# A new order of the pipeline step in a fused attention and ternary feed-forward kernel

## Chip, cores and metric

The kernel runs on one core of one Trainium2 chip. The metric is the device time of one execution in microseconds (us); less is better. The inputs and weights lie in the chip's main memory when the time starts, and the result is there when it ends.

## The reference

```
# x, ctx: (16, 128, 256) f32; 16 heads of 16; hidden width 1024
def attention(q, k, v):                    # k = v = ctx
    Q, K, V = heads(q @ Wq.T), heads(k @ Wk.T), heads(v @ Wv.T)
    p = softmax(Q @ K.T / 4, axis=-1)
    return merge(p @ V) @ Wo.T
def ffn(x):
    h = bit_linear(x, w1)                  # token rounded to 8 bits, weight to -1, 0, 1
    h = silu(conv3_over_tokens(h) + b)     # each hidden channel by itself
    return bit_linear(h, w2)
x = x + tanh(g_xattn) * attention(layernorm(x), ctx, ctx)
x = x + tanh(g_ffn)   * ffn(layernorm(x))
```

The token rounding takes the largest absolute value of a token (row) as 127. The weight rounding takes one mean absolute value for the whole matrix.

## The kernel before

Sixteen sequences of 128 tokens go through one hand-written software pipeline. Every engine has its own queue, written out in one block per engine; the queues meet in semaphores alone. The unit is a step `s` (`step` at L573 for TensorE, L837 for ScalarE, L1062 for VectorE, the loop at L367 for GpSimd). In a step four sequences are at work, with these names: b = s has its scores formed, n = s + 1 is projected, a = s - 1 is weighed with its values, d = s - 2 is normalised and rounded for the feed-forward part.

**TensorE's order in a step** (L573): `project_out(d)` (attention output times Wo, L506), `project_v(n)` (L417), `weigh(a)` (probabilities times values, L480), `x_transpose(n)` (L397), `max_transpose(b)` (row maxima, L434), `int_transpose(d-1)` (rounded tokens and their scales, L513), `project_q(n)` (L426), `unweighted_transpose(a)` (L494), the first of two hidden tiles (`hidden`, L544), `row_stage(b, 0)`, the second hidden tile, `att_transpose(a)` (L500), `project_k(n+1)` (L404), `row_stage(b, 1)`. A row stage (L441) has half of the scores of b and, between them, half of the unshifted scores of n, from which VectorE takes the row maxima. Row stage 1 waits for the exponent of row stage 0 and for VectorE's `row_max(n, 1)`, because it writes over both banks. All matrices of the attention are f32, which takes two passes a product; the profile counts each pass.

**ScalarE's order** (L837): `exponent(a, 1)` (L786), any extra work, `middle_tap` of both tiles of the step before (L817), `v_copy(n)` (L775), `sum_x`, `x_copy(n)` (L760), `u_copy(a)` (L791), `int_copy(d-1)` (two copies, L801), `q_copy(n)` (L781), `square_x`, `raw_copy` of the first tile (L812), `exponent(b, 0)`, `att_copy(a)` (L796), `k_copy(n+1)` (two copies into a buffer of keys, L765).

**VectorE's order** (L1062): `row_max(b, 0)` (L982), `residual1(d)` with the statistics of the second layernorm (L1009), `outer_taps` of one tile (L1037), `shift_q(b)` (L990), `outer_taps` of the other tile, `normalise(a)` (L1001), `row_max(n, 1)`, `quantise1(d)` (largest value and its inverse, L1019), `dequantise` of the second tile (L1029). **GpSimd's order** (L367): `norm2(d)` (L321), `dequantise` of the first tile (L345), `round1(d)` (L333), `norm1(n+1)` (L300), `x_mean` (L296).

**Hidden tiles.** From step 6 on two tiles of 128 hidden channels by 512 tokens are made per step (`TILES`, L46). The even tile is copied to SBUF by ScalarE (`raw`, L143) and multiplied with the token scales by GpSimd; the odd one VectorE multiplies out of PSUM. `ps_xqT`, `ps_deq`, `ps_w2sum` and `ps_h` lie in one bank (L159 to L174), so a hidden tile waits until `int_copy` has read its part (L564), and step 7 (`SUMS_STEP`, L47) adds the column sums of w2 in the same bank (L532), which `w2_sums_copy` (L833) takes out. Keys have three buffers (L120), values three (`VB`).

**Ends.** Before step 1 a written-out start (L637 to L662) fills the pipeline, with `project_k(2)` ahead of `row_stage(0, 1)`. The mean absolute values of w1 and w2 are summed by ScalarE in steps 1 to 4 (L903); VectorE rounds w1 and w2 in quarters (`ternary`, L1047) in steps 3 to 6, two a step, and TensorE waits before step 5 for the second mean (`mean_done`, L681). Step 15 is `last_step` (L610, L870, L1085); behind it comes a written-out mix of tiles, silu, token rounding and the second product. `keep_busy` (L392) is a product of identity matrices whose result nobody reads.

## Time and profile before

| | |
|---|---|
| Median of three runs | 236.19 us (236.08 to 236.39) |
| The profiled execution, its own time | 237.18 us |
| Its span in the profile | 235.2 us |
| Busy share: TensorE, VectorE, ScalarE, GpSimd | 92%, 81%, 69%, 52% |
| Chain that ended last: TensorE, VectorE, ScalarE | 68%, 21%, 3% |
| TensorE's granted clock, mean | 0.984 of full speed |

The span is the stretch from the first to the last instruction. A busy share is an average over stages with different limits: steps 1 to 14 last from 19.1 to 153.9 us, the last step and the written-out end from there to 235.2 us. The chain follows the work that ended last back to what released it. The stretches below are given in us from the span's start, and an instruction's duration can overlap the next one's on the same engine, so the distance of two starts tells what an instruction costs its queue.

### The profile page before, as it was taken

To read this page: it belongs to the slowest core of one execution; us is meant where nothing else is said; L and a number is where in the kernel's file an instruction comes from. 1 tells how busy PE (TensorE), PEld (TensorE's weight loads), DVE (VectorE), ACT (ScalarE), POOL (GpSimd) and SP (SyncE) were. 2 spreads that over 40 slices of the span, in tenths; PEclk is the share of its full clock that TensorE was granted. 3 is DMA by queue.
4 is the path that set the end of the run, shared out by engine and by line. 5 is a ranking of instruction groups with operands and counts; after the bars stand their busy time and mean duration, and the time that the engine had idled before them with its cause. 6 is when DMAs were issued, how large, how long until landed. Compare 5 with 4: busy or idle time off the path is not lost.

```text
span 235.2 us, 6424 instructions
## 1 busy us (share of the span) xinstructions
PE 215.8 (92%) x2439; PEld 180.1 (77%) x2452; DVE 190.4 (81%) x387; ACT 161.9 (69%) x318; POOL 122.2 (52%) x229
## 2 busy tenths in 40 slices
PE   7999999997999999999999999989985699997974
PEld 7887787886878787887878878768783588886963
DVE  4163548789798999999999999999899859999671
ACT  2557768777687888989889788667933356674741
POOL 2421326364365757668677576657567224433470
PEclk9999999999999999999999999999999589999999
DMA  5982011010110101100000000000000000111111
GB/s 168 370 270 67 3 49 38 10 46 3 45 47 3 46 3 45 40 11 22 3 3 3 3 0 3 1 3 0 3 0 0 24 25 22 47 46 45 49 52 60
DMA packets 9488, 9.86 MB, mean 42 GB/s; under 512 B 1010, under 2 KB 9202, under 8 KB 9458
## 3 DMA queue, kind: packets, MB, share of 16 engines
q1 hardware_dynamic: 9458, 9.46, 12.2%
q8 instruction: 19, 0.31, 0.6%
q14 instruction: 11, 0.09, 0.1%
HBM read 7.36 MB, written 2.10 MB: 40 GB/s over the span
## 4 chain that ended last, share of the span: by engine, by line
PE 68%; DVE 21%; issue 5%; ACT 3%; DMA 1%; POOL 1%; SPq 0%; ACTq 0%; DVEq 0%; POOLq 0%
PE ps_score L464 10%; PE ps_proj L430 8%; PE ps_proj L509 6%; PE ps_av L487 6%; PE ps_max L474 6%; PE ps_proj L422 5%; DVE zmax L1151 5%; PE ps_proj L413 4%; PE ps_h L568 4%; PE ps_av L707 4%; DVE y L1041 4%; DVE y L1044 3%; DVE smax L987 3%; PE ps_av L497 2%; PE ps_proj L401 2%
## 5 line engine op out<-in xcount | busy, mean ns | idle before, releaser
L987 DVE TENSOR_REDUCE smax<-ps_max 128x8 f32<-128x1024 f32 x31 | 37.9, 1223 | 13.9 <-PE ps_max L474 10.7
L789 ACT ACTIVATE prob<-ps_score 128x1024 f32<-128x1024 f32 x32 | 32.7, 1023 | 17.8 <-PE ps_score L464 16.9
L464 PE MATMUL ps_score<-Qs,KT 32*128 32x128 f32 x512 | 37.1, 283 | 2.0 <-DVE smax L987 0.8
L464 PEld LDWEIGHTS ps_score<-Qs,KT 32*128 32x128 f32 x512 | 31.3, 186 | 9.3 <-issue 5.0
L474 PE MATMUL ps_max<-KT,QT 32*128 32x256 f32 x248 | 35.1, 400 | 0.0
L359 POOL TENSOR_SCALAR zq<-y,zmax 128x1024 f16<-128x1024 f32 x16 | 17.9, 1119 | 29.1 <-issue 18.1
L1151 DVE TENSOR_REDUCE zmax<-y 128x1 f32<-128x1024 f32 x16 | 19.4, 1214 | 5.3 <-ACT y L935 5.3
L336 POOL TENSOR_SCALAR xn<-xn,qa 128x256 f32<-128x256 f32 x16 | 8.1, 508 | 28.1 <-DVE qa L1027 28.1
L829 ACT ACTIVATE y<-hid,conv 128x512 f32<-128x512 f32 x24 | 18.6, 807 | 4.3 <-DVE hid L1034 3.9
L707 PE MATMUL ps_av<-w2q,zqT 128*128 128x256 f16 x128 | 17.4, 281 | 4.3 <-ACT zqT L941 2.6
L474 PEld LDWEIGHTS ps_max<-KT,QT 32*128 32x128 f32 x248 | 21.1, 184 | 0.1
L1044 DVE SCALAR_TENSOR_TENSOR y<-hid,conv,y 128x508 f32<-128x508 f32 x24 | 19.6, 818 | 0.8
L941 ACT ACTIVATE zqT<-ps_proj 128x512 f32<-128x512 f32 x16 | 9.6, 598 | 15.2 <-PE ps_proj L696 15.2
L430 PE MATMUL ps_proj<-xnT,wq 128*128 128x128 f32 x128 | 18.3, 286 | 0.9 <-ACT xnT L763 0.6
L509 PE MATMUL ps_proj<-wo,attT 128*128 128x256 f32 x64 | 18.1, 405 | 1.1 <-DVE w_mean L1124 1.1
L1041 DVE SCALAR_TENSOR_TENSOR y<-hid,conv,y 128x508 f32<-128x508 f32 x24 | 18.7, 778 | 0.0
L430 PEld LDWEIGHTS ps_proj<-xnT,wq 128*128 128x128 f32 x128 | 15.6, 191 | 3.7 <-ACT xnT L763 3.5
L770 ACT ACTIVATE KT<-ps_proj,shift_row,head_mask 128x256 f32<-128x256 f32 x32 | 16.3, 563 | 2.5 <-PE ps_proj L413 2.5
L707 PEld LDWEIGHTS ps_av<-w2q,zqT 128*128 128x128 f16 x128 | 12.1, 101 | 7.2 <-DVE xres L1161 4.9
L487 PE MATMUL ps_av<-prob,V 128*32 128x128 f32 x512 | 17.3, 276 | 0.1
L350 POOL TENSOR_TENSOR hid<-raw,deq 128x512 f32<-128x512 f32 x10 | 13.1, 1311 | 7.9 <-ACT raw L815 7.9
L487 PEld LDWEIGHTS ps_av<-prob,V 128*32 128x32 f32 x512 | 13.0, 110 | 5.4 <-issue 4.5
(140 smaller groups left out, 551.9 us busy)
## 6 DMA issues: line engine op xcount, KB each, us to landing
cin<-ctxT SPq DMA_DIRECT2D x16, 128.0 KB, 2.1
xres<-x SPq DMA_DIRECT2D x16, 128.0 KB, 2.5
out<-xres SPq DMA_DIRECT2D x16, 128.0 KB, 1.7
w1f<-w1T SPq DMA_DIRECT2D x1, 1024.0 KB, 6.2
w2f<-w2T SPq DMA_DIRECT2D x1, 1024.0 KB, 8.1
wk<-wkT SPq DMA_DIRECT2D x1, 256.0 KB, 2.8
wv<-wvT SPq DMA_DIRECT2D x1, 256.0 KB, 4.4
wq<-wqT SPq DMA_DIRECT2D x1, 256.0 KB, 4.6
```

The source lines that it names most:

```text
L430: mm = pe.matmul(ps_q[:, t * P:(t + 1) * P], wq[:, k * D + t * P:k * D + (t + 1) * P], xnT[:, k * P:(k + 1) * P], start=(k == 0), stop=(k ...
L464: mm = pe.matmul(ps_score[:, i * 512 + j * P:i * 512 + (j + 1) * P], KT[b % 3][rows, j * P:(j + 1) * P], Qs[rows, j * P:(j + 1) * P], star ...
L474: mm = pe.matmul(into[:, i * 512 + t * 2 * P:i * 512 + (t + 1) * 2 * P], QT[n % 2][rows, t * P:(t + 1) * P], KT[n % 3][rows, t * 2 * P:(t ...
L487: mm = pe.matmul(ps_av[g * ROW:(g + 1) * ROW, j * P:(j + 1) * P], V[a % VB][:, h * ROW:(h + 1) * ROW], prob[g // PG][:, (g % PG * GH + j) ...
L509: mm = pe.matmul(ps_o, attT[:, t * P:(t + 1) * P], wo[:, t * D:(t + 1) * D], start=(t == 0), stop=(t == KD - 1))
L707: pe.matmul(ps_f, zqT[v % 2][:, c * P:(c + 1) * P], w2q[:, c * D:(c + 1) * D], start=(c == 0), stop=False)
L789: act.activation(prob[pair][:, :], ps_score[:, :], ACT.Exp, scale=DH ** -0.5).then_inc(exp_done, 1)
L829: act.activation(y_tile(T), by_sequence(hid[T % HB][:, :]), ACT.Identity, bias=conv[:, 4 * c + 3:4 * c + 4], scale=conv[:, 4 * c + 1:4 * c ...
L987: dve.tensor_reduce(dst, first_max(n, pair)[:, :].rearrange("p (g t e k) -> p g t e k", g=PG, t=KD, e=2), AX.X, ALU.max).then_inc(max_done, 1)
L1041: dve.scalar_tensor_tensor(y3[:, :, 1:P], h3[:, :, 0:P - 1], conv[:, 4 * c:4 * c + 1], y3[:, :, 1:P], ALU.mult, ALU.add).then_inc(tap0_don ...
L1044: dve.scalar_tensor_tensor(y3[:, :, 0:P - 1], h3[:, :, 1:P], conv[:, 4 * c + 2:4 * c + 3], y3[:, :, 0:P - 1], ALU.mult, ALU.add).then_inc( ...
L1151: dve.tensor_reduce(m[:, 0:1], z[v], AX.X, ALU.max, apply_absolute_value=True).then_inc(zmax_step, 1)
```

## The change

Keys go first and the output projection last. TensorE's step becomes `project_k(n)`, `x_transpose(n)`, `int_transpose(d-1)`, `weigh(a)`, `max_transpose(b)`, `project_q(n)`, `unweighted_transpose(a)`, tile, `row_stage(b, 0)`, tile, `att_transpose(a)`, `project_v(n)`, `project_out(a)`, `row_stage(b, 1)`. So the output projection works on a = s - 1, one step earlier, and `residual1(a)` ends VectorE's step. Keys and values have two buffers each. GpSimd multiplies both tiles of a step (all tiles under 19), from two buffers `raw`, so ScalarE copies both tiles. The absolute values of w1 are summed by VectorE in step 1 instead of by ScalarE, and the quarters of `ternary` are spread over steps 2 to 6. In step 7 the column sums come ahead of `weigh`. The gates' load and the load of Wo move up in SyncE's queue. The last step is rewritten in the same manner, with `keep_busy` in two places.

```diff
-VB = 3
+VB = 2
+KB = 2
...
-        KT = [sb(f"KT{i}", [P, KD * 2 * P]) for i in range(3)]
+        KT = [sb(f"KT{i}", [P, KD * 2 * P]) for i in range(KB)]
...
-            return T % 2 == 0 and T < FIRST_LATE
+            return T < FIRST_LATE - 1
 
         def gp_tiles(T):
-            return (min(T, FIRST_LATE) + 1) // 2
+            return min(T, FIRST_LATE - 1)
 
...
             load_x(0)
+            sp.dma_start(gate_row[:, :], gates).then_inc(gate_in, 16)
             load_w(wv, wvT, KD, wv_in)
             load_w(wq, wqT, KD, wq_in)
             load_x(1)
             load_c(1)
-            sp.dma_start(gate_row[:, :], gates).then_inc(gate_in, 16)
             load_x(2)
             load_c(2)
+            load_w(wo, woT, KD, wo_in)
             load_w(w1f, w1T, KD, w1_in)
             load_x(3)
             load_c(3)
             load_w(w2f, w2T, NC_, w2_in)
-            load_w(wo, woT, KD, wo_in)
...
                 if seq(s - 2):
                     norm2(s - 2)
-                for T in TILES.get(s, ()):
+                    round1(s - 2)
+                tiles = TILES.get(s, ())
+                for T in tiles[0:1]:
+                    dequantise(T)
+                if seq(s + 2):
+                    norm1(s + 2)
+                for T in tiles[1:2]:
                     if on_gp(T):
                         dequantise(T)
-                if seq(s - 2):
-                    round1(s - 2)
-                if seq(s + 2):
-                    norm1(s + 2)
                 if seq(s + 3):
                     gp.wait_ge(sh1_done, s + 3)
...
             def project_v(n):
-                pe.wait_ge(k_done, max(n + 1, 2))
+                if n == 0 or n == 2:
+
+                    pe.wait_ge(k_done, max(n + 1, 2))
...
-                if seq(d):
-                    project_out(d)
-                if seq(n):
+                if s == 1:
                     project_v(n)
-                if seq(a):
-                    weigh(a)
-                if seq(n):
-                    x_transpose(n)
-                max_transpose(b)
+                else:
+                    project_k(n)
+                x_transpose(n)
                 if s == SUMS_STEP:
                     w2_column_sums()
                 elif seq(d - 1):
                     int_transpose(d - 1, min(tiles, default=0))
-                if seq(n):
-                    project_q(n)
+                weigh(a)
+                max_transpose(b)
                 if s == SUMS_STEP:
                     int_transpose(d - 1, min(tiles))
-                if seq(a):
-                    unweighted_transpose(a)
+                project_q(n)
+                unweighted_transpose(a)
                 between()
                 for T in tiles[0:1]:
                     hidden(T, s - 2)
                 row_stage(b, 0)
                 for T in tiles[1:2]:
                     hidden(T, s - 2)
-                if seq(a):
-                    att_transpose(a)
-                if seq(n + 1):
-                    project_k(n + 1)
-                else:
-                    pe.wait_ge(v_done, NB)
-                    keep_busy(4, ps_k)
+                att_transpose(a)
+                if s > 1:
+                    project_v(n)
+                project_out(a)
                 row_stage(b, 1)
 
             def last_step():
                 b, a, d = NB - 1, NB - 2, NB - 3
                 T, U_ = TILES[b]
-                project_out(d)
                 hidden(T, LAST)
+                int_transpose(d - 1, T)
+                keep_busy(4, ps_av)
                 weigh(a)
                 max_transpose(b)
-                int_transpose(d - 1, T)
                 unweighted_transpose(a)
                 row_stage(b, 0)
                 y_transpose(0)
                 hidden(U_, LAST)
                 att_transpose(a)
+                keep_busy(3, ps_av)
+                project_out(a)
                 row_stage(b, 1)
...
             project_k(2)
             keep_busy(2, ps_av)
             row_stage(0, 1)
-            pe.wait_ge(gate_in, 16)
-            pe.wait_ge(ones_done, 1)
-            pe.matmul(ps_setup[:, 0:2], ones[0:1, :], gate_row[:, :], start=True, stop=True).then_inc(gate_ready, 1)
+            pe.wait_ge(wo_in, 16)
             step(1)
-            pe.wait_ge(wo_in, 16)
 
...
                 act.wait_ge(k_ready, n + 1)
-                wait(act, score_ready, PG * NP * (n - 2))
-                wait(act, max_ready, PG * NP * (n - 2))
+                wait(act, score_ready, PG * NP * (n - KB + 1))
...
-                last = TILES.get(s - 1, ())
-                if seq(a):
-                    exponent(a, 1)
-                extra()
-                for T in last:
+                exponent(a, 1)
+                if s > 1:
+                    k_copy(n)
+                x_copy(n)
+                u_copy(a)
+                for T in TILES.get(s - 1, ())[1:2]:
                     middle_tap(T)
-                if seq(n):
+                if s == 1:
                     v_copy(n)
-                if seq(n + 2):
-                    sum_x(n + 2)
-                if seq(n):
-                    x_copy(n)
-                if seq(a):
-                    u_copy(a)
                 if s == SUMS_STEP:
                     w2_sums_copy()
                 if seq(d - 1):
                     int_copy(d - 1)
-                if seq(n):
-                    q_copy(n)
+                q_copy(n)
                 if seq(n + 1):
                     square_x(n + 1)
                 for T in tiles[0:1]:
                     raw_copy(T)
+                if seq(n + 2):
+                    sum_x(n + 2)
                 exponent(b, 0)
-                if seq(a):
-                    att_copy(a)
-                if seq(n + 1):
-                    k_copy(n + 1)
+                att_copy(a)
+                for T in tiles[1:2]:
+                    raw_copy(T)
+                for T in tiles[0:1]:
+                    middle_tap(T)
+                if s > 1:
+                    v_copy(n)
+                extra()
 
             def last_step():
                 b, a, d = NB - 1, NB - 2, NB - 3
                 before, now = TILES[b - 1], TILES[b]
                 exponent(a, 1)
-                middle_tap(before[0])
                 raw_copy(now[0])
+                int_copy(d - 1)
                 u_copy(a)
                 middle_tap(before[1])
-                int_copy(d - 1)
                 exponent(b, 0)
+                att_copy(a)
                 middle_tap(now[0])
-                att_copy(a)
                 exponent(b, 1)
 
 
...
-            step(1, weight_sum(0, 0))
-            act.wait_ge(gate_ready, 1)
-            act.activation(gate[:, :], ps_setup[:, 0:2], ACT.Tanh).then_inc(gate_done, 1)
-            step(2, weight_sum(0, 1))
+            step(1)
+            step(2, weight_sum(0))
             act.wait_ge(mean_done, 1)
-            step(3, weight_sum(1, 0))
-            step(4, weight_sum(1, 1))
+            step(3, weight_sum(1))
+            step(4)
             step(5, first_weights(0))
...
-                tiles, last = TILES.get(s, ()), TILES.get(s - 1, ())
-                if seq(b):
-                    row_max(b, 0)
-                if seq(d):
-                    residual1(d)
+                last = TILES.get(s - 1, ())
+                row_max(b, 0)
                 for T in last[0:1]:
                     outer_taps(T)
                 extra(0)
                 shift_q(b)
+                if seq(d):
+                    quantise1(d)
+                if seq(a):
+                    normalise(a)
                 for T in last[1:2]:
                     outer_taps(T)
-                if seq(a):
-                    normalise(a)
                 if seq(n):
                     row_max(n, 1)
-                if seq(d):
-                    quantise1(d)
-                for T in tiles[1:2]:
-                    dequantise(T)
                 extra(1)
+                if seq(a):
+                    residual1(a)
 
             def last_step():
                 b, a, d = NB - 1, NB - 2, NB - 3
                 before, now = TILES[b - 1], TILES[b]
                 row_max(b, 0)
-                residual1(d)
                 outer_taps(before[0])
                 shift_q(b)
+                quantise1(d)
+                normalise(a)
                 outer_taps(before[1])
-                normalise(a)
-                quantise1(d)
+                remainder(d - 1)
                 dequantise(now[1])
-                remainder(d - 1)
+                residual1(a)
                 outer_taps(now[0])
...
+            def first_sums(k):
+                if k == 0:
+                    dve.wait_ge(w1_in, 16)
+                dve.tensor_reduce(abs_sum[:, 2 * k:2 * k + 1], w1f[:, k * HID:(k + 1) * HID], AX.X, ALU.add,
+                                  apply_absolute_value=True).then_inc(abs_done[0], 1)
+
+            step(1, first_sums)
...
-            step(2, lambda k: weight_scale(0) if k == 1 else None)
-            step(3, pieces(0, w1f, w1q, 0, wq1_step, w1q_done))
-            step(4, pieces(2, w1f, w1q, 0, wq1_step, w1q_done, scale=1))
-            step(5, pieces(0, w2f, w2q, 1, wq2_step, w2q_done))
+            w1_args = (w1f, w1q, 0, wq1_step, w1q_done)
+            w2_args = (w2f, w2q, 1, wq2_step, w2q_done)
+
+            def second(k):
+                if k == 1:
+                    weight_scale(0)
+                    ternary(0, *w1_args)
+
+            def third(k):
+                ternary(1 + k, *w1_args)
+
+            def fourth(k):
+                if k == 0:
+                    ternary(3, *w1_args)
+                else:
+                    weight_scale(1)
+                    ternary(0, *w2_args)
+
+            def fifth(k):
+                ternary(1 + k, *w2_args)
+
+            def sixth(k):
+                if k == 0:
+                    ternary(3, *w2_args)
+
+            step(2, second)
+            step(3, third)
+            step(4, fourth)
+            step(5, fifth)
             dve.wait_ge(small_in, 16)
-            step(6, pieces(2, w2f, w2q, 1, wq2_step, w2q_done))
+            step(6, sixth)
...
-            residual1(NB - 2)
...
```

The hunks left out change only the waits that go with this (buffers, the bank of the hidden tiles, the order at the start: the gates' product and its `Tanh` now come before `project_q(0)`), and behind the last step `hidden(20)` goes first, with four `keep_busy` products ahead of `weigh(NB - 1)`.

## Rows read from the trace of the kernel before

**Rows 1.** Stretches cut at the starts of steps 2, 7 and 8:

```profile
27.68:75.75 48.07, 45.63 (x597) 38.11 (x594) 38.16 (x88) 36.13 (x82) 22.70 (x51) 1.00 0.10 29
75.75:86.47 10.72, 10.20 (x132) 8.38 (x129) 10.21 (x20) 8.61 (x20) 7.24 (x13) 1.00 0.09 27
```

**Rows 2.** Timeline of TensorE (start, length, idle before) in step 10, a steady one:

```profile
105.74 1.13 PE L509 MATMUL ps_proj<-wo,attT 128*128 128x256 f32 x4
...
107.66 1.08 PE L487 MATMUL ps_av<-prob,V 128*32 128x128 f32 x32
...
108.95 0.38 PE L438 MATMUL ps_score<-ident,smax 128*128 128x128 f32 x2
...
109.58 0.97 PEld L430 LDWEIGHTS ps_proj<-xnT,wq 128*128 128x128 f32 x8 [0.22 <-ACT xnT L763]
110.58 0.60 PE L497 MATMUL ps_av<-ident,U 128*128 128x128 f32 x4
...
111.54 0.38 PE L464 MATMUL ps_score<-Qs,KT 32*128 32x128 f32 x2
...
113.30 1.06 PE L413 MATMUL ps_proj<-cin,wk 128*128 128x128 f32 x8
114.28 0.38 PE L464 MATMUL ps_score<-Qs,KT 32*128 32x128 f32 x2
...
115.37 0.48 PE L509 MATMUL ps_proj<-wo,attT 128*128 128x256 f32 x1
```

**Rows 3.** Waits of TensorE, summed (us, times, longest):

```profile
PE ps_proj L509 <- DVE w_mean L1124: 1.1, 1, 1.1
```

**Rows 4.** Timeline of ScalarE in step 10:

```profile
106.87 1.51 ACT L829 ACTIVATE y<-hid,conv 128x512 f32<-128x512 f32 x2
...
109.43 0.59 ACT L794 ACTIVATE U<-ps_av 128x512 f32<-128x512 f32 x1
...
110.17 0.38 ACT L809 ACTIVATE deq<-ps_h,w_mean 128x128 f32<-128x128 f32 x1
110.78 0.38 ACT L784 ACTIVATE QT<-ps_proj 128x256 f32<-128x256 f32 x1 [0.23 <-PE ps_proj L430]
...
112.85 1.02 ACT L789 ACTIVATE prob<-ps_score 128x1024 f32<-128x1024 f32 x1 [0.60 <-PE ps_score L464]
```

**Rows 5.** Timelines of SyncE, TensorE and ScalarE at the start:

```profile
4.11 0.33 SPq L268 DMA_DIRECT2D gate_row<-gates  x1
...
19.10 1.13 PE L422 MATMUL ps_proj<-wv,cin 128*128 128x256 f32 x4
...
17.58 1.02 ACT L770 ACTIVATE KT<-ps_proj,shift_row,head_mask 128x256 f32<-128x256 f32 x2
...
19.22 1.02 ACT L789 ACTIVATE prob<-ps_score 128x1024 f32<-128x1024 f32 x1 [0.62 <-PE ps_score L464]
```

**Rows 6.** Timeline of GpSimd in step 10:

```profile
106.22 0.19 POOL L307 TENSOR_SCALAR var<-x_squares 128x1 f32<-128x1 f32 x1
...
108.36 0.51 POOL L323 TENSOR_SCALAR var<-mv 128x1 f32<-128x1 f32 x1
...
110.48 0.97 POOL L330 TENSOR_SCALAR xn<-xres,rstd,shift 128x256 f32<-128x256 f32 x1
...
114.80 0.48 POOL L336 TENSOR_SCALAR xn<-xn,qa 128x256 f32<-128x256 f32 x1 [1.20 <-DVE qa L1027]
```

**Rows 7.** VectorE's search for the token maximum, step 10:

```profile
113.90 0.41 DVE L1021 TENSOR_REDUCE qa<-xn 128x1 f32<-128x256 f32 x1
```

**Rows 8.** GpSimd's multiplications, shortest, median and longest (ns):

```profile
L350 POOL TENSOR_TENSOR hid<-raw,deq x10: 1266/1269/1692, 72.7 to 159.6; 128x512 f32<-128x512 f32 x10
```

**Rows 9.** Timeline of VectorE in the last step and behind it:

```profile
155.18 0.48 DVE L1011 SCALAR_TENSOR_TENSOR xres<-ps_proj,gate,xres 128x256 f32<-128x256 f32 x1
...
156.25 0.71 DVE L1041 SCALAR_TENSOR_TENSOR y<-hid,conv,y 128x508 f32<-128x508 f32 x1
...
166.69 1.22 DVE L1151 TENSOR_REDUCE zmax<-y 128x1 f32<-128x1024 f32 x1 [0.47 <-ACT y L935]
```

47 lines of the change are left out of this document (22 added, 25 removed).

## The prediction

> **What bounds the kernel now.** I read the share of busy time and the chain that ended last first: TensorE has most of both. Then the stretches step by step, because an average hides which step has room: steps 2 to 6 take 48.07 us together, though no hidden tile is made before step 6, and step 7 takes 10.72 [rows 1]. Then TensorE's timeline in a steady step, where the distance of two starts is what a stage costs. It reads: output projection with values 1.92, `weigh` with `x_transpose` 1.29, both small transposes up to the queries 0.63, queries 1.00, the U transpose with a tile 0.96, row stage, tile and `att_transpose` 1.76, keys 0.98, row stage 1.09; 9.63 in all [rows 2]. The only wait in it is 0.2 before the queries, for ScalarE's copy [rows 2]. So TensorE's own work is 9.43, and in steps 6 and 8 to 14 an order alone can give back 0.2 a step. The room is earlier, where 1.1 is one wait for the second weight mean [rows 3].
>
> I split the sums so: a pass of a 128-column transpose is 0.11, so four for U 0.44, two for the maxima 0.22, `int_transpose` 0.21, `att_transpose` 0.22, `x_transpose` 0.28; the first tile 0.52, the second 0.44, `row_stage(b, 0)` 1.10, values or output projection 0.96 each, `weigh` 1.01.
>
> **How the new step runs.** Count from the start of `project_k(n)`. ScalarE gets a product some 0.04 after its modelled end (queries: 110.58 is the next start, 110.78 the copy's) [rows 2, 4].
>
> *Steps 8 to 14.* `weigh` ends at 0.98 + 1.29 + 0.21 = 2.48. TensorE comes to the first tile at 2.48 + 0.22 + 1.00 + 0.44 = 4.14. But the tile shares its bank with what `int_copy` reads, and ScalarE now has `u_copy`, a middle tap and both int copies between the end of `weigh` and the tile: 0.11 to hand over, 0.74 for U and the first int copy, 0.75 for the tap (half of 1.51), 0.38 for the scales, 0.05 back, in all 2.03 [rows 4]; ready at 4.51. A wait of 0.37 that the old order did not have, since there V, xT and the taps lay ahead of `weigh`'s end. After it nothing is late: `att_copy` follows the exponent, 0.21 + 1.02 + 0.38 = 1.61 after the row stage [rows 4], against tile, transpose and values, 1.62. The step is 9.43 + 0.37 = 9.80, 0.17 over the old one; seven of them **+1.2**.
>
> *Steps 2 to 6.* Without a tile TensorE is at `project_out(a)` 1.18 after the row stage, but the copy needs 1.61: 0.43 wait. The copied queries come 0.20 + 0.38 + 0.05 after their product, 0.63 against 0.44: 0.19 wait. Steps 3 and 5: 2.48 + 0.22 + 1.00 + 0.63 + 1.10 + 1.61 + 0.96 + 1.09 = 9.09. Step 2 has no `int_transpose` but the weight mean (four passes, 0.44) in place of the query wait, 9.13; step 4 both, 9.34; step 6 has tiles but no tap yet, 9.43. Together 46.08 against 48.07: **-2.0**. More than half is the second mean, which now comes ahead of a `ternary` and not behind it [rows 3].
>
> *Step 7.* The column sums (eight passes, 0.9 after `project_k`'s eight) go ahead of `weigh`, and `int_transpose` has to wait until they are copied out. `weigh` ends at 3.17, then U 0.5, the tap 0.75, the copy 0.38 and the two hand-overs: 4.96. TensorE is there at 3.39 and stands 1.57. 9.43 + 0.9 + 1.57 = 11.90 against 10.72 [rows 1]: **+1.2**.
>
> *Step 1.* Two key buffers: `k_copy(2)` writes the buffer of sequence 0 and so waits for all its scores, the event that started the exponent at 19.22; before it ran at 17.58 [rows 5]. It comes first in ScalarE's queue, so it ends at 20.24, and `project_v(2)`, which waits for it and stood at 19.10, starts at 20.29. The exponent and `weigh` queue behind. From there 0.96 + 1.29 + 0.22 + 1.00 + 0.63 + 1.10 + 1.61 + 0.96 + 1.09 = 8.86, so step 2 starts at 29.15 and not at 27.68: **+1.5**. Each step now holds `project_out(a)` where the old one held `project_k(n+1)`, so the two starts compare like with like.
>
> *GpSimd.* It gets a second multiplication, 1.27 and 0.1 between instructions [rows 8]. Its round of one step: `norm1` and mean 2.14, `norm2` 3.09 (110.48 + 0.97 - 108.36), VectorE's `quantise1` for which it stands still 0.90, `round1` 1.05 (114.80 to the next `norm1`, 9.63 behind 106.22), two multiplications 2.74 [rows 6 to 8], with a hand-over 10.0. That is 0.2 over TensorE's 9.80. Lower bound nothing, as `quantise1` has slack before the row maximum that TensorE needs; upper 7 times 0.2. I take half, **+0.7**. `norm1` stays early enough for `x_transpose`: it has nearly a step of cover.
>
> *VectorE* gives up a multiplication and is covered. w1's sums go to it in step 1, where it is idle half the time; should w1 come late the shift would stand behind them, for which no row speaks. *ScalarE* gets a copy of 0.6 and still has idle time.
>
> *Loads.* The gates' issue takes 0.33 of SyncE's queue [rows 5] and moves ahead of wv, wq, x1 and c1; Wo's moves ahead of w1. All are awaited later than they land, so nothing; were the cover of x1 gone, 0.33. The gates' product moves from the front of step 1 to an idle place: nothing.
>
> *The end.* `residual1(13)`, 1.07 of VectorE (155.18 to 156.25), leaves the last step, so `shift_q(15)` comes up to that earlier; I take 0.6, because the four `keep_busy` products hold `weigh` back. But three more and `project_out(14)` now stand ahead of `row_stage(15, 1)`: 0.73 (six of the passes of keys) and 0.96. The exponent, the table load and the first silu hang on that stage, and VectorE's first token maximum waited for silu already, at 166.69 [rows 9]. Later by 1.69 - 0.6 = **+1.1**; bounds 0.6 and 1.7, and -1.07 if VectorE's work alone sets the end.
>
> **The sum:** 1.5 - 2.0 + 1.2 + 1.2 + 0.7 + 1.1 = +3.7. The profiled execution's span of 235.2 becomes 238.9 and its own 237.18 becomes 240.9; it lies 1.0 over the median of the runs shown, to which I add the same: 236.19 + 3.7 = **239.9**. Its own range, with half of each wait and the bounds of the end and of GpSimd: 237.5 to 242.
>
> **Where a rule of the skill bears on it.** GpSimd's multiplication took 1.27 nearly always, and 1.69 the one time that VectorE's taps ran beside it (159.6) [rows 8]; the scaling in `norm2` shows 0.97 under a tap [rows 6]. The Trainium skill (SBUF — State Buffer, Who interferes with whom) says why: a VectorE instruction with two SBUF inputs and a GpSimd one that reads SBUF lock each other out for the whole instruction. The trace agrees with its direction. By it the second multiplication is dearer than an idle GpSimd makes it look, and the taps can stand behind it too.
>
> **Rivals.**
> 1. *The lock makes GpSimd the bound* (0.14). If one multiplication a step lasts 1.69, the round is 10.0 + 0.42 = 10.4; seven steps at 0.64 over 9.80 are 4.5 in place of 0.7: 243.7. For it: new places beside the taps. Against: `norm2` then meets fewer taps, and the maxima have PSUM inputs. It decides from the point where the round is over 9.8.
> 2. *Faster: ScalarE's copies are never late in steps 2 to 14* (0.19). Its queue has 0.6 idle before the exponent [rows 4], and if the chain from `weigh` to the tile takes under 1.66 and not 2.03, TensorE runs packed: 8.70, 8.47, 8.91, 8.47 and 9.43 for steps 2 to 6 (-4.1), step 7 10.33 (-0.4), 9.43 for seven steps (-1.4). With step 1 and the end, +1.5 and +1.1, that is -3.3: 232.9. For it: 0.37 is a small difference of two sums. Against: each term is a row's length, and the exponent with its copy takes 1.61 whatever the queue does.
> 3. *It cancels* (0.07): the end is paid by VectorE's work (-1.07 for +1.1) and step 7's copy is not late (0 for +1.2): 3.7 - 2.2 - 1.2 = +0.3, 236.5.
>
> **How the numbers follow.** The forecast has 0.60. A measurement of this kernel tells 0.2% (0.5 us) from no change. Faster: rival 2 and a seventh of rival 3, 0.20; same: the rest of rival 3 less a little, 0.05; slower 0.75. The range from 235.9 to 243.0 holds the forecast, rival 3 and the lower part of rival 1 and leaves out rival 2, some 0.2.
>
> **What the new profile would show.** Right: `project_v(2)` at 20.3 and `k_copy(2)` after the scores; step 7 close to 11.9 with TensorE idle before `int_transpose`; steady steps of 9.8 to 10.0 with the wait before the first tile on ScalarE's scale copy; no wait on the weight mean; silu(0) later against the start of step 15. Wrong: steady steps under 9.63, or a tile that waits for nothing; then the ScalarE chain is mis-sized. GpSimd without idle time but for `quantise1` would speak for rival 1.

## The result, and the profile after

The changed kernel takes 241.53 us (median of four runs, 241.27 to 241.62) against 236.29 for the kernel before on the same chip. The ratio is 1.0213, 95% interval 1.0185 to 1.0241: slower by 5.2 us. The profiled execution of the changed kernel took 241.27 with a span of 239.5, 4.3 over the span before.

Page of the changed kernel: busy shares, the chain that ended last, the group of GpSimd's multiplications (count, busy us, mean ns, idle before).

```profile
PE 214.4 (90%) x2453; PEld 177.8 (74%) x2466; DVE 187.3 (78%) x378; ACT 163.5 (68%) x323; POOL 133.8 (56%) x238
...
PE 63%; DVE 19%; issue 8%; ACT 7%; DMA 1%; POOL 1%; SPq 0%; ACTq 0%; DVEq 0%; POOLq 0%
...
L351 POOL TENSOR_TENSOR hid<-raw,deq 128x512 f32<-128x512 f32 x19 | 26.8, 1409 | 1.0 <-ACT raw L814 0.9
```

TensorE has lost share of the chain, and ScalarE and "issue" have gained it: TensorE works as long as before but stands more often. A view by stretch says where. These are the changed kernel's stretches, cut at `project_v(2)` and at the starts of steps 2, 7, 8 and 15 (stretch, length, then busy time and count of PE, PEld, DVE, ACT and POOL, granted clock, DMA share, GB/s).

```profile
20.68:29.64 8.96, 7.71 (x106) 6.12 (x106) 5.92 (x9) 4.59 (x11) 1.77 (x5) 1.00 0.11 31
29.64:76.21 46.57, 45.22 (x598) 37.23 (x595) 39.47 (x90) 36.18 (x82) 25.36 (x56) 1.00 0.11 30
76.21:88.45 12.24, 10.52 (x132) 8.26 (x129) 9.44 (x17) 9.32 (x21) 7.65 (x14) 1.00 0.09 25
88.45:158.35 69.90, 66.00 (x844) 52.65 (x849) 58.13 (x112) 58.81 (x127) 55.56 (x88) 1.00 0.04 11
```

Against [rows 1]: steps 2 to 6 take 46.57 in place of 48.07, step 7 12.24 in place of 10.72. The last row holds seven steps of 9.98; before they took 9.63. Next TensorE's timeline in step 1, in the steady step that starts at 108.42, and in step 7 (start, length, idle before and its releaser).

```profile
20.68 1.10 PE L427 MATMUL ps_proj<-wv,cin 128*128 128x256 f32 x4 [1.37 <-ACT KT L769]
...
27.49 1.13 PE L512 MATMUL ps_proj<-wo,attT 128*128 128x256 f32 x4 [1.13 <-ACT attT L798]
...
81.28 0.27 PE L533 MATMUL ps_h<-ident,xq 128*128 128x128 bf16 x2 [1.45 <-issue]
...
110.96 0.44 PE L443 MATMUL ps_score<-ident,smax 128*128 128x128 f32 x2
111.23 1.06 PE L435 MATMUL ps_proj<-xnT,wq 128*128 128x128 f32 x8
112.12 0.60 PE L500 MATMUL ps_av<-ident,U 128*128 128x128 f32 x4
113.05 0.11 PEld L572 LDWEIGHTS ps_h<-xqT,w1q 128*128 128x128 bf16 x2 [0.56 <-ACT deq L808]
113.28 0.38 PE L572 MATMUL ps_h<-xqT,w1q 128*128 128x512 bf16 x1 [0.56 <-ACT deq L808]
```

The last of these lines needs care. A tile is two passes, and the line holds one (x1): this trace has no record of the first pass, in any of steps 8 to 14. Its weight load shows when the tile really started, at 113.05. In the trace of experiment 5, whose steps are as long, both passes are recorded, and the wait reads 0.33 and not 0.56:

```profile
113.71 0.60 PE L573 MATMUL ps_h<-xqT,w1q 128*128 128x512 bf16 x2 [0.33 <-ACT deq L809]
```

The forecast new waits are all there: the values behind `k_copy(2)`, the output projection behind `att_copy`, `int_transpose` in step 7 behind the sums' copy (the view names no releaser, experiment 2 shows it), the first tile behind the scale copy. One was not forecast. At the end of step 7 row stage 1 waits for VectorE's row maxima, which stand behind a tap that met a multiplication of GpSimd and took 1.64 in place of 0.75:

```profile
87.36 0.38 PE L467 MATMUL ps_score<-Qs,KT 32*128 32x128 f32 x2 [0.22 <-DVE smax L983]
...
84.44 1.64 DVE L1040 SCALAR_TENSOR_TENSOR y<-hid,conv,y 128x508 f32<-128x508 f32 x1
...
84.14 1.39 POOL L351 TENSOR_TENSOR hid<-raw,deq 128x512 f32<-128x512 f32 x1 [0.94 <-ACT raw L814]
```

And ScalarE's side of two of the forecast waits:

```profile
19.52 1.02 ACT L769 ACTIVATE KT<-ps_proj,shift_row,head_mask 128x256 f32<-128x256 f32 x2 [1.66 <-PE ps_score L467]
20.43 1.02 ACT L788 ACTIVATE prob<-ps_score 128x1024 f32<-128x1024 f32 x1
...
111.17 0.60 ACT L793 ACTIVATE U<-ps_av 128x512 f32<-128x512 f32 x1 [0.26 <-PE ps_av L490]
111.67 0.80 ACT L828 ACTIVATE y<-hid,conv 128x512 f32<-128x512 f32 x1
112.37 0.37 ACT L806 ACTIVATE xqT<-ps_h 128x256 bf16<-128x256 bf16 x1
112.64 0.37 ACT L808 ACTIVATE deq<-ps_h,w_mean 128x128 f32<-128x128 f32 x1
112.89 0.39 ACT L783 ACTIVATE QT<-ps_proj 128x256 f32<-128x256 f32 x1
```

In the first two lines the keys' copy waits for the scores and holds the exponent back, where [rows 5] had the copy at 17.58 and the exponent at 19.22. In the others U, the tap and two copies run without a gap, and TensorE waits for the second copy. GpSimd in the same step:

```profile
108.14 1.27 POOL L351 TENSOR_TENSOR hid<-raw,deq 128x512 f32<-128x512 f32 x1
...
113.11 0.48 POOL L337 TENSOR_SCALAR xn<-xn,qa 128x256 f32<-128x256 f32 x1 [1.11 <-DVE qa L1023]
...
114.53 1.69 POOL L351 TENSOR_TENSOR hid<-raw,deq 128x512 f32<-128x512 f32 x1
```

One of the two multiplications takes 1.69 in each of steps 8 to 13, as the one under a tap had [rows 8]. The only idle time is 1.11 for the token maximum. Where GpSimd is the bound (experiment 10) that wait is 0.93, so by these two rows I estimate 0.18 to spare here. Last, the first token maximum behind the last step, which was at 166.69 [rows 9]:

```profile
172.37 1.22 DVE L1169 TENSOR_REDUCE zmax<-y 128x1 f32<-128x1024 f32 x1 [2.28 <-ACT y L931]
```

From there the changed kernel needs 67.1 us to the end of its span and the kernel before 68.5. The clock says why. TensorE alone, the kernel before first, then the changed one (stretch, length, busy, granted clock, DMA share, GB/s):

```profile
184.00:188.00 4.00, 3.60 (x17) 0.50 0.11 35
188.00:192.00 4.00, 4.00 (x27) 0.72 0.01 2
```

```profile
184.00:188.00 4.00, 2.47 (x23) 1.00 0.00 0
188.00:192.00 4.00, 1.92 (x11) 0.68 0.00 0
192.00:196.00 4.00, 4.00 (x32) 0.89 0.11 37
```

Around the start of the second product TensorE falls to 1.2 GHz (0.50) for a while; before it lay idle for most of 180 to 184 (1.09 busy of 4.00). The stretch at the lower clock was shorter in this execution after the change. The profiled kernel with two multiplications below (experiment 10) has the long one, 68.4 us from the token maximum to the end, and its partner with one multiplication the short one, 67.2. So some 1.2 us of the difference of two single spans can be this.

### The profile page after: what moved, and what is told of

Its sections match the earlier page's. It is cut to its first block, busy times and chain, and to the rows that moved or that the text cites. A ratio compares the mean times of both kernels' runs of the same rounds, so it can differ in the third digit from the quotient of the medians.

```text
span 239.5 us, 6464 instructions
## 1 busy us (share of the span) xinstructions
PE 214.4 (90%) x2453; PEld 177.8 (74%) x2466; DVE 187.3 (78%) x378; ACT 163.5 (68%) x323; POOL 133.8 (56%) x238
## 4 chain that ended last, share of the span: by engine, by line
PE 63%; DVE 19%; issue 8%; ACT 7%; DMA 1%; POOL 1%; SPq 0%; ACTq 0%; DVEq 0%; POOLq 0%
PE ps_score L467 10%; PE ps_av L490 7%; PE ps_proj L416 7%; PE ps_proj L512 6%; PE ps_max L477 5%; DVE zmax L1169 5%; DVE y L1037 4%; PE ps_proj L427 4%; PE ps_h L572 4%; DVE y L1040 4%; PE ps_proj L435 3%; PE ps_av L707 3%; ACT y L828 2%; DVE xres L1179 2%; PE ps_av L398 2%
## 5 line engine op out<-in xcount | busy, mean ns | idle before, releaser
L351 POOL TENSOR_TENSOR hid<-raw,deq 128x512 f32<-128x512 f32 x19 | 26.8, 1409 | 1.0 <-ACT raw L814 0.9
L828 ACT ACTIVATE y<-hid,conv 128x512 f32<-128x512 f32 x24 | 19.5, 814 | 4.9 <-DVE hid L1030 3.9
L707 PE MATMUL ps_av<-w2q,zqT 128*128 128x256 f16 x128 | 16.6, 273 | 4.3 <-ACT zqT L937 2.6
L1040 DVE SCALAR_TENSOR_TENSOR y<-hid,conv,y 128x508 f32<-128x508 f32 x24 | 18.9, 788 | 0.9
L991 DVE SCALAR_TENSOR_TENSOR Qs<-ps_score,max_row,QT 128x256 f32<-128x256 f32 x32 | 14.0, 477 | 6.5 <-PE ps_score L443 6.4
L1037 DVE SCALAR_TENSOR_TENSOR y<-hid,conv,y 128x508 f32<-128x508 f32 x24 | 18.9, 786 | 0.0
L416 PE MATMUL ps_proj<-cin,wk 128*128 128x128 f32 x128 | 18.3, 286 | 0.0
L427 PE MATMUL ps_proj<-wv,cin 128*128 128x256 f32 x64 | 16.5, 381 | 1.4 <-ACT KT L769 1.4
L435 PE MATMUL ps_proj<-xnT,wq 128*128 128x128 f32 x128 | 17.0, 275 | 0.0
```

What stands on the lines that cost most here:

```text
L351: gp.tensor_tensor(hid[T % HB][:, :], raw[T % 2][:, :], deq[:, G * GT:(G + 1) * GT], ALU.mult).then_inc(scaled_gp, 1)
L416: mm = pe.matmul(ps_k[:, t * P:(t + 1) * P], wk[:, k * D + t * P:k * D + (t + 1) * P], cin[n % CB][:, k * P:(k + 1) * P], start=(k == 0), ...
L427: mm = pe.matmul(ps_v, cin[n % CB][:, k * P:(k + 1) * P], wv[:, k * D:(k + 1) * D], start=(k == 0), stop=(k == KD - 1))
L1037: dve.scalar_tensor_tensor(y3[:, :, 1:P], h3[:, :, 0:P - 1], conv[:, 4 * c:4 * c + 1], y3[:, :, 1:P], ALU.mult, ALU.add).then_inc(tap0_don ...
L1040: dve.scalar_tensor_tensor(y3[:, :, 0:P - 1], h3[:, :, 1:P], conv[:, 4 * c + 2:4 * c + 3], y3[:, :, 0:P - 1], ALU.mult, ALU.add).then_inc( ...
```

## The experiments

All ratios are against the kernel before, run beside it on the same chip (its medians there lie between 236.29 and 236.85). The table reads, for each kernel: start of step 2, length of step 7, length of each of steps 8 to 14, start of the first token maximum, median time. Its first four columns come from TensorE's and VectorE's timelines; the beginning of the program shifts by up to 0.7 from one execution to the next (`project_k(2)` starts between 16.55 and 17.27). So two kernels are best compared by the distance from the start of step 2 to the token maximum, 142.73 in the changed kernel.

| kernel | step 2 | step 7 | steps 8 to 14 | token max | median | ratio |
|---|---|---|---|---|---|---|
| before | 27.68 | 10.72 | 9.63 | 166.69 | 236.29 | 1 |
| after | 29.64 | 12.24 | 9.98 | 172.37 | 241.53 | 1.0213 |
| 1 three keys | 28.21 | 12.24 | 9.98 | 170.92 | 240.36 | 1.0197 |
| 2 sums' copy first | 29.72 | 10.63 | 9.98 to 10.32 | 172.08 | 241.37 | 1.0224 |
| 3 scales before tap | 30.09 | 11.66 | 9.80 to 10.31 | 172.96 | 242.18 | 1.0248 |
| 4 row stage first | 29.66 | 12.24 | 9.98 | 171.72 | 241.05 | 1.0205 |
| 5 one multiplication | 30.29 | 12.24 | 9.98 | 173.01 | 241.84 | 1.0220 |
| 6 = 2, 3 and 5 | 30.16 | 10.46 | 9.81 | 169.87 | 239.35 | 1.0110 |
| 7 = 1 to 5 | 28.45 | 10.46 | 9.81 | 167.51 | 236.78 | 1.0018 |
| 8 old step, two mult. | 28.16 | 12.14 | 10.81 to 11.23 | 178.90 | 248.82 | 1.0497 |
| 9 = 7, tap after queries | 28.89 | 11.11 | 9.47 to 9.76 | 167.79 | 236.92 | 1.0027 |
| 10 = 9, two mult. | 28.18 | 11.11 | 9.75 to 10.29 | 169.68 | 239.89 | 1.0153 |
| 11 = 9, maxima first | 28.41 | 10.63 | 9.47 to 9.76 | 166.86 | 236.11 | 0.9990 |
| 12 = 11, tap after raw | 28.55 | 10.35 | 9.48 | 165.24 | 234.13 | 0.9888 |

**1. Keys in three buffers again.**

```diff
-KB = 2
+KB = 3
```

> The new kernel with three key buffers instead of two. Theory: with two, k_copy(2) waits for all scores of sequence 0 and project_v(2) stands 1.37 us for it; with three that wait is gone, project_v(2) starts near 19.4 in place of 20.7, all later stages are 1.2 to 1.4 earlier with steps of unchanged length, and the time is 240.2 (0.5% less than the new kernel's 241.5). Rival: the first step is held by the exponent and its att_copy (1.13 before project_out(0)) whatever the keys do; then step 2 starts where it did, near 29.6, and the time stays at 241.5.

Measured: 240.36 us, ratio 1.0197 (1.0142 to 1.0252), 1.2 under the changed kernel. `project_v(2)` starts at 19.20, step 2 at 28.21 and not 29.64, and all later steps keep their lengths. The missing buffer is the cause of that part of step 1, and it is paid once. The trace shows this and the ratio doesn't, since its interval holds 1.0213: one of the four executions took 242.57.

**2. The column sums' copy ahead of U's in step 7.**

```diff
                 x_copy(n)
+                if s == SUMS_STEP:
+                    w2_sums_copy()
                 u_copy(a)
...
-                if s == SUMS_STEP:
-                    w2_sums_copy()
```

> The new kernel with the copy of w2's column sums ahead of u_copy and the middle tap in ScalarE's queue of step 7. Theory: TensorE's wait of 1.45 before int_transpose in step 7 is this copy standing behind U and the tap; ScalarE is idle for 0.91 just where the copy now goes, so the wait goes, about 0.4 comes back before the first tile as in a steady step, step 7 takes 11.0 to 11.2 and not 12.24, time 240.4. Rival: the step is held by VectorE or GpSimd (quantise1 waits there too), then step 7 stays over 11.9 and the time at 241.3 or more.

Measured: 241.37 us (1.0224, 1.019 to 1.0258), no gain. Step 7 fell from 12.24 to 10.63, as it should, but steps 10 to 13 rose to 10.20 to 10.32. GpSimd in a step of 10.3 of that kernel:

```profile
117.73 1.28 POOL L351 TENSOR_TENSOR hid<-raw,deq 128x512 f32<-128x512 f32 x1
118.98 0.67 POOL L299 TENSOR_SCALAR minus_mean<-x_total 128x1 f32<-128x1 f32 x1
119.73 0.68 POOL L324 TENSOR_SCALAR var<-mv 128x1 f32<-128x1 f32 x1
...
124.44 1.69 POOL L351 TENSOR_TENSOR hid<-raw,deq 128x512 f32<-128x512 f32 x1
```

The two operations on 128x1 took 0.23 and 0.22 in the changed kernel and take 0.67 and 0.68 here, since they now fall on VectorE's taps. GpSimd's round becomes 10.3 and VectorE waits for its second layernorm. The time that TensorE stood in step 7 had given GpSimd a lead: its second multiplication started 0.69 before step 8 in the changed kernel (87.76 against 88.45) and 0.19 before it here (86.72 against 86.91), and by step 10 it starts 0.55 behind the step's start. That this lead is what kept GpSimd's layernorm clear of the taps is my reading of these rows; no run changed the lead alone. I had not seen that.

**3. The rounded tokens and their scales ahead of the tap.**

```diff
                 u_copy(a)
-                for T in TILES.get(s - 1, ())[1:2]:
-                    middle_tap(T)
...
                 if seq(d - 1):
                     int_copy(d - 1)
+                for T in TILES.get(s - 1, ())[1:2]:
+                    middle_tap(T)
                 q_copy(n)
```

> The new kernel with int_copy ahead of the middle tap of the second tile in ScalarE's queue. Theory A, the wait of 0.5 before the first tile is ScalarE's alone: it vanishes, steps 8 to 14 take 9.45 to 9.5 and not 9.98, and step 7 loses the tap's 0.7 only where it stands ahead of the sums' copy (it still does not: the copy stays ahead of int_copy, so the tap leaves its path, about 0.7 less); time 237.2 to 237.6. Theory B, GpSimd is the next bound: its round has only 0.2 of slack (quantise1 starts 0.23 after norm2 ends), so the steps stop at 9.75 to 9.8 with quantise1 waiting for GpSimd, and the time is 239.0 to 239.5.

Measured: 242.18 us (1.0248, 1.0221 to 1.0274), no gain. Whether it is slower than the change the runs don't tell: from the start of step 2 to the token maximum it takes 142.87 against 142.73. The first tile now waits for nothing and steps 8 and 9 are 9.80, but steps 11 to 13 are 10.31, VectorE waiting for the second layernorm up to 1.0 a step. Taking away TensorE's wait laid GpSimd bare; both theories missed the time.

**4. The last row stage ahead of the output projection.**

```diff
                 att_transpose(a)
-                keep_busy(3, ps_av)
-                project_out(a)
                 row_stage(b, 1)
+                project_out(a)
```

(in `last_step`.)

> The new kernel with row_stage(15, 1) ahead of project_out(14) in the last step, and the three keep_busy products there left out. Theory: the chain row stage, exponent, table load, silu(0) starts 1.5 to 1.7 earlier, VectorE's idle 2.28 before the first token maximum shrinks to 0.6 to 0.8, everything behind follows; time 240.0. Rival 1: VectorE's own work (residual1(14) now later, taps, tile 20) takes the place at once, the gain is under 0.5, time 241.1. Rival 2: the keep_busy products held TensorE's clock and their loss gives a stretch at 1.2 GHz before the last phase; then the clock of the stretch from 165 to 190 is under 1.

Measured: 241.05 us (1.0205, 1.0173 to 1.0237). VectorE's view at the first token maximum:

```profile
171.72 1.22 DVE L1168 TENSOR_REDUCE zmax<-y 128x1 f32<-128x1024 f32 x1 [1.08 <-ACT y L930]
```

It waits 1.08 and not 2.28, but starts only 0.65 earlier: the order costs about half of what I expected. The rest is in ScalarE's queue, at the last exponent:

```profile
166.73 0.81 ACT L827 ACTIVATE y<-hid,conv 128x512 f32<-128x512 f32 x1 [1.03 <-POOL hid L351]
167.45 1.00 ACT L787 ACTIVATE prob<-ps_score 128x1024 f32<-128x1024 f32 x1
```

The exponent stands behind a tap that waits for GpSimd's multiplication (165.43, 1.27 long). It starts at 167.45, 0.59 before its 168.04 in the changed kernel, where it had waited for the scores; the table load and the silu follow it. VectorE waits less mainly because its own work, with `residual1(14)` 0.56 later (167.47 for 166.91), ends later, and that costs nothing: it still waits for silu.

**5. GpSimd multiplies the even tiles only.**

```diff
-            return T < FIRST_LATE - 1
+            return T % 2 == 0 and T < FIRST_LATE
...
-                for T in tiles[1:2]:
-                    raw_copy(T)
```

(and `dequantise` of the second tile back in VectorE's step behind `row_max(n, 1)`.)

> The new kernel with GpSimd multiplying only the even tile, VectorE the odd one behind row_max(n, 1), as before the change. Theory: two limits lie close together in the new steps, GpSimd's round (10.3 once its lead is used up, as the two last experiments showed) and the ScalarE chain ahead of the first tile (9.98). Taking the multiplication off GpSimd alone moves neither the 9.98 nor step 7's 12.24: 241.2 to 241.6. Rival: GpSimd's multiplication already costs in the 9.98 (through the tap or the copies it delays); then the steps fall to 9.8 or less and the time to 240.2 or less.

Measured: 241.84 us (1.022, 1.0193 to 1.0247), steps 9.98 and 12.24 to the hundredth. Alone the second multiplication costs nothing: TensorE's wait for ScalarE covers it.

**6. Experiments 2, 3 and 5 together.**

> As the experiment before, with both changes of ScalarE's order that gained nothing with two multiplications: int_copy ahead of the middle tap, and the sums' copy right behind x_copy in step 7. Theory: GpSimd's round was what swallowed them; with one multiplication it is near 9.0, so steps 8 to 14 take 9.45 to 9.6, step 7 10.4 to 10.7, and the time is 236.3 to 237.3. Rival: VectorE, with the odd multiplication back, or another wait takes over at once; then the steps stay at 9.8 or more and the time over 238.5.

Measured: 239.35 us (1.011, 1.0082 to 1.0138). Steps are 9.81 throughout; the rise to 10.3 is gone with the second multiplication. But it is not 9.45. TensorE's only remaining wait in such a step:

```profile
111.80 0.38 PE L467 MATMUL ps_score<-Qs,KT 32*128 32x128 f32 x2 [0.26 <-ACT QT L784]
```

The tap has to stand somewhere in ScalarE's queue; ahead of `q_copy` it delays the copied queries, which the row stage needs.

**7. All repairs: 1 to 5 together.**

> All repairs together: three key buffers, the sums' copy early, int_copy ahead of the tap, one multiplication on GpSimd, and row_stage(15, 1) ahead of project_out(14) without the keep_busy products. Theory: the gains add, 1.3 from the keys, 1.5 from step 7, 3 to 3.6 from the steps, 0.5 from the end: 234.6 to 235.6, under the kernel before (236.3). Rival: the repaired order is at best as good as the old one, 236.3 or more.

Measured: 236.78 us, ratio 1.0018 (0.9994 to 1.0042), the kernel before within the error. By the ratios the five edits together are worth 1.95%, 4.6 us; one by one they came to 0.16, -0.11, -0.35, 0.08 and -0.07%, 0.7 us the wrong way. These single ratios are uncertain by 0.3 to 0.6%, and by the medians the five sum to 0.66%, 1.6 us the right way. The traces are finer. From the start of step 2 to the token maximum, experiments 2, 3 and 5 alone take 142.36, 142.87 and 142.72, which sum to a gain of 0.2 over the change's 142.73; together (experiment 6) they take 139.71, a gain of 3.0. The other two simply add: the keys save their 1.4 before step 2, and the last row stage 0.65 (139.06 here), where alone it saved 0.67.

**8. The old step, with both multiplications on GpSimd.** This kernel keeps three buffers of keys and three of values and has one `raw`, as before.

```diff
-            return T % 2 == 0 and T < FIRST_LATE
+            return T < FIRST_LATE - 1
...
                     norm1(s + 2)
+                for T in TILES.get(s, ())[1:2]:
+                    if on_gp(T):
+                        dequantise(T)
```

> The kernel before, its step order kept, with one part of the change alone: GpSimd multiplies both tiles (the odd one behind norm1, from the same raw buffer) and ScalarE copies both. Theory: GpSimd's round becomes the bound here too, 10.0 to 10.3 a step in place of 9.63 once its idle 2.1 is gone, in steps 6 and 8 to 14 about 3 to 5 in all: 239.0 to 241.0. Rival: the old order has the slack for it (2.1 of idle time against 1.4 of work) and VectorE's relief helps; then the time stays within 0.5 of 236.3.

Measured: 248.82 us (1.0497, 1.0462 to 1.0532), far over. From the timelines of one step, TensorE, ScalarE, VectorE and GpSimd in turn:

```profile
116.26 1.16 PE L432 MATMUL ps_proj<-xnT,wq 128*128 128x128 f32 x8 [1.61 <-ACT xnT L766]
...
114.46 0.81 ACT L832 ACTIVATE y<-hid,conv 128x512 f32<-128x512 f32 x1 [1.68 <-POOL hid L350]
...
113.17 1.79 DVE L1046 SCALAR_TENSOR_TENSOR y<-hid,conv,y 128x508 f32<-128x508 f32 x1
...
113.15 1.27 POOL L350 TENSOR_TENSOR hid<-raw,deq 128x512 f32<-128x512 f32 x1
```

The step of 11.21 (steps 8 to 12) is the old 9.63 plus, nearly, the 1.61 of the first line. In the old order both taps stand ahead of `x_copy` in ScalarE's queue, so a late multiplication goes straight to TensorE's queries. The last two lines start together, and VectorE pays: 1.79 for a tap of 0.73. So in the old order the second multiplication, made from one `raw`, costs 5%. The single `raw` is a part of that price that this run doesn't separate.

**9. All repairs, with the tap behind the queries' copy.**

```diff
-                for T in TILES.get(s - 1, ())[1:2]:
-                    middle_tap(T)
                 q_copy(n)
+                for T in TILES.get(s - 1, ())[1:2]:
+                    middle_tap(T)
```

> The kernel with all repairs (keys in three buffers, w2's column sums copied out early, the token scales' copy ahead of the middle tap, one GpSimd multiplication a step, the last row stage ahead of the output projection), with one thing more: the middle tap now stands behind q_copy and not ahead of it. My theory: the steady steps of 9.81 in that kernel come from the copied queries, which sat behind the tap of 0.75 and let TensorE stand about 0.35 before the first row stage; the remaining few hundredths are copies of the attention. With the tap behind the queries' copy steps 8 to 14 fall to 9.45 to 9.55, TensorE's own work, step 7 to about 10.3, and the total to 234.3 to 235.3 us, which is below the kernel before. Rival 1: VectorE is the bound of that step, since its second taps wait for the middle tap, now 0.4 later, and row_max(n, 1) comes behind them; then the wait appears before row stage 1 and steps stay at 9.7 or more, total 236.3 to 237. Rival 2: the queries were not the cause (the copy waits for TensorE, not the reverse): steps stay at 9.8, and nothing changes.

Measured: 236.92 us (1.0027, 0.9999 to 1.0055). Steps 8 to 12 are 9.75 and not 9.5; the wait went from the row stage to the second tile (0.19, for `raw`), and step 7 grew from 10.46 to 11.11. Step 7 from the timelines of VectorE and GpSimd:

```profile
81.35 0.96 DVE L1035 SCALAR_TENSOR_TENSOR y<-hid,conv,y 128x508 f32<-128x508 f32 x1
82.35 1.84 DVE L1038 SCALAR_TENSOR_TENSOR y<-hid,conv,y 128x508 f32<-128x508 f32 x1
84.11 1.21 DVE L981 TENSOR_REDUCE smax<-ps_max 128x8 f32<-128x1024 f32 x1
...
82.38 1.27 POOL L351 TENSOR_TENSOR hid<-raw,deq 128x512 f32<-128x512 f32 x1 [0.59 <-ACT raw L814]
```

Counted from the start of step 7, the second tap starts at 6.90 in place of experiment 7's 6.63, and the multiplication at 6.93. There the tap took 0.76 and the multiplication 1.69; here the tap takes 1.84 and the multiplication 1.27. The row maxima stand behind the tap, and TensorE behind them (0.41 before row stage 1).

**10. The same with two multiplications.**

> The same kernel, with GpSimd multiplying both tiles of a step again, as in the change; only this differs. My theory: with TensorE's own waits gone GpSimd's round sets the steps, which was 10.3 in both kernels where one of those waits had been taken away: steps 8 to 14 go to 10.2 to 10.35 as soon as GpSimd has used up what it was ahead, the total is 3.5 to 5.5 us above the kernel with one multiplication, 239 to 240.5 us, and GpSimd shows no idle time but for quantise1. Rival: the 10.3 was ScalarE's doing (its second raw copy and the tap that waits for GpSimd), and with the tap later there is room: then steps stay below 9.8 and the second multiplication costs under 1.5 us in all.

Measured: 239.89 us (1.0153, 1.0125 to 1.0181), 3.0 over experiment 9. Steps 8 and 9 are 9.75, step 10 is 10.07, steps 11 to 13 are 10.29, step 14 is 9.95. Timelines of TensorE, VectorE and GpSimd:

```profile
124.62 0.38 PE L467 MATMUL ps_score<-Qs,KT 32*128 32x128 f32 x2 [0.46 <-DVE smax L982]
...
116.69 1.21 DVE L1036 SCALAR_TENSOR_TENSOR y<-hid,conv,y 128x508 f32<-128x508 f32 x1
...
120.46 0.42 DVE L1016 TENSOR_REDUCE qa<-xn 128x1 f32<-128x256 f32 x1 [1.00 <-POOL xn L331]
...
121.36 0.48 POOL L337 TENSOR_SCALAR xn<-xn,qa 128x256 f32<-128x256 f32 x1 [0.93 <-DVE qa L1022]
...
117.33 0.66 POOL L299 TENSOR_SCALAR minus_mean<-x_total 128x1 f32<-128x1 f32 x1
```

The ring is visible: GpSimd's layernorm late, VectorE's search for the maximum behind it, the row maxima behind that, TensorE last. From the start of step 2 to the token maximum it takes 141.50 us and experiment 9 takes 138.90, so the second multiplication costs 2.6 here. The profiled spans differ by 3.1, because this execution began 0.7 earlier and had the longer stretch at the lower clock, 1.2. In the 3.0 of the medians a part is that clock too: all four executions of this kernel have a mean granted clock of 0.984 or 0.985, and the five of experiment 9 that have it show a median of 237.67, 2.2 less.

**11. The row maxima ahead of the second taps.**

```diff
-                for T in last[1:2]:
-                    outer_taps(T)
                 if seq(n):
                     row_max(n, 1)
                 for T in TILES.get(s, ())[1:2]:
                     dequantise(T)
+                for T in last[1:2]:
+                    outer_taps(T)
```

> The kernel with all repairs and the middle tap behind q_copy (236.9 us, step 7 11.11, steps 8 to 14 9.75), with one edit in VectorE's queue: row_max(n, 1) and the second tile's multiplication go ahead of the outer taps of the second tile. In step 7 of that kernel the second taps took 0.96 and 1.84 instead of 0.74 and 0.76, beside GpSimd's multiplication, and the row maxima stood behind them. My theory: those 1.3 us of lock reached TensorE through row_max alone, so step 7 falls from 11.11 to 10.3 to 10.5, while steps 8 to 14, where the taps met no multiplication, stay at 9.75 (their 0.19 before the second tile is the copy raw, behind the tap and the square). Total 236.0 to 236.4. Rival: the lock only moves: the taps now lie where GpSimd multiplies in every step, VectorE's queue gets 0.7 to 1.0 longer per step, residual1 comes late for the next row_max, and steps 8 to 14 rise to 9.9 or more, 237.5 to 239.

Measured: 236.11 us (0.999, 0.9968 to 1.0012). Step 7 is 10.63, steps 8 to 12 are 9.75, the taps 0.74 and 0.75 again: placed behind the maxima they miss the multiplication.

**12. And the tap behind the copy of the first tile.**

```diff
                 q_copy(n)
-                for T in TILES.get(s - 1, ())[1:2]:
-                    middle_tap(T)
...
                 for T in tiles[0:1]:
                     raw_copy(T)
-                if seq(n + 2):
-                    sum_x(n + 2)
+                for T in TILES.get(s - 1, ())[1:2]:
+                    middle_tap(T)
                 exponent(b, 0)
...
                     v_copy(n)
+                if seq(n + 2):
+                    sum_x(n + 2)
```

> As the run beside it, and the middle tap moved once more, behind raw_copy of the first tile, with sum_x moved to the end of ScalarE's step to make room. My theory: the last wait of TensorE in the steady step, 0.19 before the second tile, goes, and steps 8 to 14 are 9.50 to 9.60, step 7 10.2 to 10.4; the total is 234.6 to 235.3 us, 0.4% to 0.8% under the kernel before. The maxima no longer stand behind the taps, so the later tap costs VectorE's queue nothing that TensorE waits for. Rival: the later taps meet GpSimd's multiplication in every step, and VectorE, at 0.7 to 1.0 us longer per step, becomes the bound: steps of 9.9 to 10.3 and 237.5 to 240. A second rival: exponent and att_copy come later by the tap and the wait moves to project_out: steps stay at 9.7 to 9.8.

Measured: 234.13 us (233.85 to 234.43), ratio 0.9888 (0.9863 to 0.9913): faster than both kernels. Its stretches, cut at the starts of steps 2, 7, 8 and 15, columns as above:

```profile
28.55:75.12 46.57, 45.21 (x598) 37.22 (x595) 40.05 (x91) 35.73 (x81) 24.72 (x56) 1.00 0.11 29
75.12:85.47 10.35, 10.30 (x133) 8.27 (x130) 8.68 (x16) 8.51 (x20) 6.42 (x11) 1.00 0.10 29
85.47:151.80 66.33, 65.96 (x844) 52.98 (x847) 61.30 (x120) 55.78 (x120) 47.26 (x81) 1.00 0.04 12
```

In the last row TensorE is busy for 65.96 of 66.33: steps of 9.48 with next to nothing left to take by order. The 1.5 us by which the first token maximum is earlier than in the kernel before are 0.9 lost up to step 2, 1.5, 0.4 and 1.1 won in these three stretches, and 0.7 lost in the last step. The 0.7 in the last step has the cause found in experiment 4: the last exponent stands behind a tap that waits 1.07 for GpSimd.

The change's two ideas part here: the change with the repairs and without the second multiplication is good for 2.3 us in the medians. Not all of that is TensorE's order. Of the 1.5 in steps 2 to 6, 1.15 lie in step 4 (46.32 to 56.86 before, 10.54; 9.39 now), where the wait for the second weight mean is gone [rows 3]; that is the work of the earlier mean and the spread `ternary`, which no run took back alone.

## Why the prediction was right, step by step

The forecast was 239.9 with a range to 243.0 and a chance of 0.75 for slower; measured is 241.53. The sign and the places of the waits held, and the size was 1.5 us short. By its terms, from the profile of the changed kernel:

| term | predicted | measured |
|---|---|---|
| step 1 | +1.5 | +1.96 |
| steps 2 to 6 | -2.0 | -1.50 |
| step 7 | +1.2 | +1.52 |
| steps 8 to 14 with GpSimd | +1.2 +0.7 | +2.46 |
| last step to the token maximum | +1.1 | +1.24 |
| from there to the end | 0 | -1.4 |
| sum | +3.7 | +4.3 |

**Step 1** was right in its cause: experiment 1 takes back 1.43 of it. `project_v(2)` came at 20.68, 0.4 after the 20.29 I gave. The start of the program itself was 0.24 later in this execution (`project_k(2)` at 16.62 for 16.38), and from the copy's modelled end (20.54) to TensorE's start I had 0.05 where the rows say 0.14. The stretch from there is 8.96 for 8.86, by the output projection below.

**Steps 8 to 14** are 9.98 and not 9.80, and three small sizes make the difference. TensorE's own work I had at 9.43, and experiment 12 shows 9.48: from the start of the output projection to the row stage behind it are 1.06 us, where I had taken 0.96 from its old place ahead of the values, and the values give back 0.05. `weigh` ends 2.54 after the step's start and not 2.48. And the chain from there to the tile is 2.09 (110.96 to the weight load at 113.05) and not 2.03: the hand-over from TensorE to ScalarE took 0.21 (110.96 to 111.17) where I had 0.11, the four instructions between took 1.84 for 1.87, and the hand-over back 0.04 (the scales' modelled end at 113.01 to 113.05) for 0.05. TensorE, packed, would be at the tile 4.15 after the step's start (by experiment 12's rows), so the wait is 0.5 in place of 0.37, and 9.48 + 0.50 = 9.98. The 0.56 that the view prints is too much, since the first pass has no record, and its 0.33 in experiment 5 is too little, since it counts from a modelled end.

**Steps 2 to 6** are 9.22, 9.24, 9.39, 9.24 and 9.48, against 9.13, 9.09, 9.34, 9.09 and 9.43. In step 3, 0.10 of the 0.15 is the output projection again; row stage 0 comes another 0.1 late, and the copy of the attention comes 0.05 sooner than I had it. The removed wait for the second weight mean was right.

**Step 7** I had at 11.90, and it is 12.24. The stall before `int_transpose` was right: 1.57 forecast, and 1.6 from where experiment 2 has it packed (0.28 after the small transpose's start at 79.40) to 81.28. What I put at nothing was the wait for the row maxima. From the output projection to row stage 1 are 1.35 us there, and 1.06 in every other step, so 0.29 of the 0.34 is the lock between VectorE's tap and GpSimd's multiplication. It is not the second multiplication's doing: experiment 5 has the same 1.35.

**GpSimd.** I gave it +0.7 as the bound over a TensorE at 9.80. In the changed kernel it costs nothing: experiment 5 takes the second multiplication out and no step moves. The 1.9 for steps 8 to 14 was 0.5 short because 1.2 was missing in TensorE's work and wait (0.18 a step) and 0.7 stood there for nothing: two wrong terms that half cancel, which is luck.

**Rival 1** (the lock makes GpSimd the bound, round 10.4) got 0.14 and its time of 243.7 did not come. Its mechanism is real and lies right behind: as soon as TensorE's waits are taken away, the round is 10.3 (experiments 2, 3 and 10, measured against the 10.4 of the sum). "It decides from the point where the round is over 9.8" was wrong by the step's real length, 9.98, and, as I read experiment 2, by the lead that step 7's stall gives GpSimd. And the lock did cost TensorE where this rival didn't look, 0.29 in step 7. The Trainium skill (SBUF — State Buffer, Who interferes with whom) says that the order of issue decides which of the two engines waits. The traces here agree: the multiplication took 1.69 where the tap ran first (114.32 against 114.53 in the changed kernel), and the tap 1.79 where the multiplication was 0.02 ahead of it (experiment 8). In experiment 9 the two starts, 0.03 apart, say the reverse, and VectorE still paid with 1.84; that is too close for the rows to order.

**Rival 2** (ScalarE's copies never late) needed a chain under 1.66; it is 2.09. What it describes, steps of 9.43, is what experiment 12 reaches at 9.48 by moving the tap out of the chain. **Rival 3** needed the end and step 7 both covered; neither was.

**The end** was right at +1.24 for +1.1. Its explanation was half right: experiment 4 moves the projection and the `keep_busy` products away and gains 0.65 at the token maximum, not 1.7. With the projection out of the way the last exponent hangs on ScalarE's tap and that on GpSimd's multiplication, a path that the prediction didn't have. The 0.6 for the removed `residual1(13)` was right: `shift_q(15)` comes 3.11 after the start of step 15 (161.46 against 158.35) and came 3.75 after it before.

**The last phase** I had at nothing. In work it is, but the lower clock around 184 to 192 lasts shorter in this execution, by 1.4 of span. That is the main reason why the spans differ by 4.3 and the medians by 5.2: the profiled execution of the kernel before, with the long stretch, lies 1.0 over its median, and that of the changed kernel doesn't. Executions alike in this would differ by about 5.2, so the +3.7 is short by 1.5 and not by 0.6.

## What to carry to other kernels

A part that costs nothing when it is undone alone may be covered by another part's wait: price it again with the cover gone. Here the places of two copies and one multiplication gave 0.2 us when each was undone alone, and 3.0 us together; the second multiplication cost nothing in the changed kernel and 2.2 to 2.6 us once the waits over it were gone. When a small operation of a copying engine stands between a product and the next one that needs it, ask of every queue place which consumer is nearest; the tap was moved three times (0.33, 0.26, 0.19, 0 of TensorE's wait by the views) before it lay where nobody waited for it. And before a wait is explained, see that its instruction is complete in the trace: a count of x1 where the program has two, with a weight load 0.23 us earlier, had made a wait of 0.33 into one of 0.56, and a hand-over of 0.04 into one of 0.27.

## What was unexpected

GpSimd and VectorE shut each other out also where one of them has almost nothing to do: operations of GpSimd on 128x1 went from 0.23 and 0.22 to 0.66 and 0.68 when they fell under a tap, so a step's round grew by 0.3 without one more instruction. A shift of 0.3 us of VectorE's tap against the step sufficed to turn a tap of 0.76 into one of 1.84 (experiment 9). The state is kept from step to step: once GpSimd's layernorm starts under the taps, TensorE's step settles at 10.3 and stays there through step 13.
